# Group norm in token order, and x turned by crossbar DMA, in an attention layer for 64 images

## The chip, the cores and the metric

The kernel runs on one core of a Trainium2 chip. The core has TensorE (PE in the rows; PEld is its weight load), VectorE (DVE), ScalarE (ACT), GpSimd (POOL), SyncE (SP, which here only issues DMAs) and 16 DMA engines. The metric is device time in microseconds (us) of one execution, lower is better.

## What is computed

Group norm over x, attention with LoRA and decomposed relative positions for each of 64 images of 14 x 14 tokens, a projection, and x added on. Cut to what matters:

```python
# x: (64, 14, 14, 768); 12 heads of 64; G = 32 groups of 24 channels
g = x.reshape(64, 14, 14, 32, 24)
m = mean(g, axis=(1, 2, 4)); s = var(g, axis=(1, 2, 4))
t = ((g - m) / sqrt(s + 1e-5)).reshape(x.shape)
qkv = t @ qkv_w.T + qkv_b          # new_q = t @ la_q.T @ lb_q.T is added to q, new_v likewise to v
attn = (q * scale) @ k.T + rel_h(q) + rel_w(q)     # 196 x 196 per image and head
out = x + softmax(attn) @ v @ proj_w.T + proj_b
```

## The kernel before

Images go in pairs (32 rounds, `pairs`), 392 columns each. Products with f32 precision are made of three f16 products (high x high, low x high, high x low), so each operand has a `_hi` and a `_lo` half. `prepare` merges LoRA into the weights and splits them; `attend` is the main loop. It keeps x of one pair in `x_sb` as 98 token partitions x 4 blocks x 768 channels.

What each engine does in which order is written out by hand in the tables `PE_ORDER`, `ACT_ORDER`, `DVE_ORDER`, `SP_ORDER`: an entry (kind, old, k) stands for step k of that kind for the pair of the round less `old` (-1 is the next pair, 1 the one before). Each engine goes through its list in order and waits on semaphores; nothing overtakes. The kinds:

- S k, P k (k = 0 to 11: a pair of heads of one image): score product, and product of probabilities and v. Between them on DVE and ACT: the row maximum (S, L769), exponentials (N on ACT, L682), reciprocal and splitting (N and T, L777 to L789), then a crossbar DMA on SP that turns the split probabilities (`turned<-split`, T, L528).
- Q, K, V k (k = 0 to 5): projections of 18 products (L556), read by ACT and DVE. R: relative positions (L578). Y, Z: output projection (L623), turned back (L629), added to x (`y_sb`, L803); LY and ST load and store `y_sb`, which has YS = 3 slots; `yT` has 2.
- LD (ACT's queue): the load of `x_sb` for a later pair.
- X k (k = 0 to 5): PE turns x, four f32 transposes each (L637); ACT copies them to `xT`, channels on partitions (L708); DVE takes bn_stats of each image (L808).
- M, G: bn_aggr (L813), then two products with `gmean` average over a group's partitions (L642), DVE derives mean and variance; POOL raises to the power -0.5 on [128, 2] (L722).
- H, L: DVE normalizes `xT` (L833), ACT writes `xn_hi` (L712), DVE `xn_lo` (L839). Q 0 of a pair waits for them.

PSUM results other than scores and P go through a ring of 5 banks; a product waits until the result five places before it was read.

## Time and profile before

| | |
|---|---|
| median of 3 runs | 3372.74 us (3370.44 to 3375.27) |
| the profiled execution, its own time | 3373.03 us |
| its span in the trace | 3371.3 us |
| PE, DVE, ACT, POOL busy | 98%, 75%, 62%, 1% of the span |
| queue of SP's DMAs (q1), share of the 16 DMA engines | 49.8% |

The profile is one execution. Busy time of PE is that of overlapping products: a product of 392 columns is listed with 0.33 us, but the next begins 0.17 later. The chain of waits tells the time that each really adds.

### The profile page before, as it was taken

How to read it: one execution, taken by the hardware profiler on the slowest of the kernel's cores; microseconds unless marked ns; L12 is line 12 of the kernel's file. 1: busy time of each engine (PE TensorE's matmuls, PEld its weight loads, DVE VectorE, ACT ScalarE, POOL GpSimd, SP SyncE). 2: the span in 40 equal slices, each digit the busy share in tenths (PEclk: the TensorE clock that was granted, in tenths of full speed). 3: DMA queues.
4: the chain of work that ended last, by engine and by line, in shares of the span. 5: the costliest groups of instructions: out<-in, count | busy, mean ns of one | idle time of the engine just before them, and what ended most of it. 6: DMA issues, size and time to landing. Idle time of an engine off the chain costs nothing.

```text
span 3371.3 us, 80148 instructions
## 1 busy us (share of the span) xinstructions
PE 3297.2 (98%) x31984; PEld 2130.7 (63%) x31984; DVE 2528.2 (75%) x5970; ACT 2098.2 (62%) x5651; POOL 35.8 (1%) x65
## 2 busy tenths in 40 slices
PE   7689999999999999999999999999999999999998
PEld 4456666666666666666666666666666666666665
DVE  7577777777777777777777777777777777777764
ACT  2466666666666666666666666666666666666664
POOL 0000000000000000000000000000000000000000
PEclk9799999999999999999999999999999999999999
DMA  3145664555555556565555555555565555565554
GB/s 128 42 96 109 120 122 103 115 113 112 118 121 107 113 112 114 116 121 107 110 116 113 112 123 118 101 117 111 110 127 120 100 118 108 111 126 122 103 106 105
DMA packets 1091412, 376.13 MB, mean 112 GB/s; under 512 B 916696, under 2 KB 1071320, under 8 KB 1091040
## 3 DMA queue, kind: packets, MB, share of 16 engines
q1 hardware_dynamic: 1075206, 333.63, 49.8%
q10 hardware_dynamic: 15834, 37.37, 3.9%
q8 instruction: 254, 4.16, 0.5%
q14 instruction: 118, 0.97, 0.1%
HBM read 86.60 MB, written 38.54 MB: 37 GB/s over the span
## 4 chain that ended last, share of the span: by engine, by line
PE 94%; DVE 2%; ACT 1%; issue 0%; DMA 0%; POOL 0%; SPq 0%; POOLq 0%; DVEq 0%
PE ring L556 51%; PE ring L623 17%; PE score L599 9%; PE o_ps L613 7%; PE ring L578 3%; PE ring L637 3%; PE ring L629 3%; ACT prob L682 1%; PE ring L642 0%; PE ring L563 0%; DVE split L789 0%; DVE row_max L769 0%; DVE rel_sb L762 0%; DVE split L781 0%; DVE rel_sb L756 0%
## 5 line engine op out<-in xcount | busy, mean ns | idle before, releaser
L556 PE MATMUL ring<-xn_hi,w_hi 128*128 128x392 f16 x3456 | 1143.2, 331 | 4.8 <-DVE xn_lo L839 4.6
L556 PE MATMUL ring<-xn_lo,w_hi 128*128 128x392 f16 x3456 | 1139.8, 330 | 0.0
L556 PE MATMUL ring<-xn_hi,w_lo 128*128 128x392 f16 x3456 | 1139.3, 330 | 0.5 <-issue 0.5
L682 ACT ACTIVATE prob<-score,neg_max,exp_scale 98x196 f32<-98x196 f32 x1536 | 769.8, 511 | 252.9 <-DVE neg_max L773 245.4
L769 DVE TENSOR_REDUCE row_max<-score 98x4 f32<-98x784 f32 x384 | 373.3, 972 | 273.2 <-PE score L599 272.1
L789 DVE SCALAR_TENSOR_TENSOR split<-prob,row_inv,split 98x196 f16<-98x196 f32 x1536 | 545.0, 417 | 7.8
L556 PEld LDWEIGHTS ring<-xn_hi,w_hi 128*128 128x128 f16 x3456 | 342.3, 99 | 260.7 <-issue 7.7
L556 PEld LDWEIGHTS ring<-xn_hi,w_lo 128*128 128x128 f16 x3456 | 338.8, 98 | 237.9 <-issue 3.6
L556 PEld LDWEIGHTS ring<-xn_lo,w_hi 128*128 128x128 f16 x3456 | 338.9, 98 | 208.3 <-issue 1.9
L623 PE MATMUL ring<-o_hi,w_hi 128*128 128x392 f16 x1152 | 380.2, 330 | 1.4 <-DVE o_lo L798 1.4
L623 PE MATMUL ring<-o_lo,w_hi 128*128 128x392 f16 x1152 | 379.8, 330 | 0.0
L623 PE MATMUL ring<-o_hi,w_lo 128*128 128x392 f16 x1152 | 379.6, 330 | 0.0
L690 ACT ACTIVATE split<-prob,row_inv 98x196 f16<-98x196 f32 x768 | 310.3, 456 | 52.9 <-DVE row_inv L777 52.1
L682 ACT ACTIVATION_READ_ACCUMULATOR prob<-score,neg_max,exp_scale 98x1 f32 x1536 | 306.2, 199 | 0.0
L658 ACT ACTIVATE q_hi<-ring,bias 128x392 f16<-128x392 f32 x192 | 112.1, 584 | 297.8 <-PE ring L556 297.8
L777 DVE RECIPROCAL row_inv<-row_sum 98x4 f32<-98x4 f32 x384 | 68.0, 177 | 290.6 <-ACT prob L682 290.6
L613 PE MATMUL o_ps<-turned,v_tok 98*64 98x196 f16 x4608 | 269.5, 252 | 4.0 <-DMA turned<-split 4.0
L701 ACT ACTIVATE yT<-ring,bias,y_scale 128x392 f32<-128x392 f32 x192 | 130.1, 678 | 220.6 <-PE ring L623 220.6
L599 PE MATMUL score<-k_hi,q_hi 64*98 64x196 f16 x1536 | 205.7, 264 | 19.7 <-DVE k_lo L736 12.3
L781 DVE TENSOR_SCALAR split<-prob,row_inv 98x196 f16<-98x196 f32 x768 | 213.0, 320 | 14.3 <-DVE row_inv L777 0.8
L613 PEld LDWEIGHTS o_ps<-turned,v_tok 98*64 98x64 f16 x4608 | 184.8, 109 | 56.1 <-DMA turned<-split 4.3
L697 ACT ACTIVATE o_hi<-o_ps,bias 128x392 f16<-128x392 f32 x192 | 112.7, 587 | 141.3 <-PE o_ps L613 141.3
(118 smaller groups left out, 4896.7 us busy)
## 6 DMA issues: line engine op xcount, KB each, us to landing
y_sb<-in_x SPq DMA_DIRECT2D x192, 196.0 KB
out<-y_sb SPq DMA_DIRECT2D x192, 196.0 KB
x_sb<-in_x ACTq DMA_DIRECT2D x31, 1176.0 KB
rel_q<-rel_sb SPq DMA_DIRECT2D x128, 122.5 KB, 2.4
stage<-in_L_conv_qkv_w SPq DMA_DIRECT2D x3, 2304.0 KB, 15.4
turned<-split SPq DMA_TRANSPOSE x384, 4.2
rel_q<-rel_sb SPq DMA_DIRECT2D x128, 24.5 KB, 1.9
v_tok<-v_split SPq DMA_TRANSPOSE x192, 3.4
```

The costliest lines, as they stand in the source:

```text
L556: last = T.matmul(ring[:, bank, 0:NT], w[:, c, 128 * j:128 * j + 128], xx[:, par, c, :], start=(c == 0 and part == 0), stop=(c == CT - 1 a ...
L599: last = T.matmul(score[0:HALF, head, to], stat[rows, qs], kk[rows, :], start=(part == 0), stop=(part == 3))
L613: last = T.matmul(o_ps[rows, c0:c0 + TOK], v_tok[0:HALF, hp % 2, vv, 2 * image + kh, rows], turned[0:HALF, image, pp, head, :, kh, 0:HALF] ...
L623: last = T.matmul(ring[:, bank, 0:NT], w[:, c, 128 * j:128 * j + 128], oo[:, par, c, :], start=(c == 0 and part == 0), stop=(c == HP - 1 a ...
L658: last = A.activation(to, ring[:, bank, 0:NT], ACT.Identity, bias=bias[:, j:j + 1])
L682: last = A.activation(prob[:, head, half, :], score[0:HALF, head, TOK * half:TOK * half + TOK], ACT.Exp, bias=neg_max[:, k % 2, i:i + 1], ...
L690: last = A.activation(split[0:HALF, k % 2, 0, 0, half, :, 0:HALF], prob[:, 0, half, :].rearrange("p (a k) -> p a k", a=2), ACT.Copy, scale ...
L697: A.activation(o_hi[:, par, hp, :], o_ps[:, 0:NT], ACT.Identity, bias=bias[:, 2 * CT + hp:2 * CT + hp + 1]).then_inc(o_hi_made, 1)
L701: A.activation(yT[:, k % 2, :], ring[:, bank, 0:NT], ACT.Identity, bias=bias[:, 3 * CT + k:3 * CT + k + 1], scale=y_scale[:, :]).then_inc( ...
L769: V.tensor_reduce(row_max[:, k % 2, :], score[0:HALF, :, 0:2 * TOK].rearrange("p a (b k) -> p a b k", b=2), AX.X, ALU.max).then_inc(row_ma ...
L781: last = V.tensor_scalar(split[0:HALF, k % 2, 0, 1, half, :, 0:HALF], prob[:, 1, half, :].rearrange("p (a k) -> p a k", a=2), row_inv[:, k ...
L789: last = V.scalar_tensor_tensor(split[0:HALF, k % 2, 1, head, half, :, 0:HALF], prob[:, head, half, :].rearrange("p (a k) -> p a k", a=2), ...
```

## The change

The statistics are taken in token order, before x is turned, and the turning moves from PE to the DMA queue. A k (k = 0, 1: one image) sums each group's 24 channels of two blocks for each token partition on DVE; product G 0 with `gmean` (now 98 x 98, all 1/(24 x 196)) adds over partitions and leaves the mean on every partition; B k subtracts it in `x_sb`; U k squares on ACT into `squares` (which shares memory with `xs`, as do `qw_hi` and `qw_lo`); D k sums the squares; product G 1 gives the 64 variances on 64 partitions, one element each; POOL takes the power there; E puts them on a diagonal; product G 2 with ones spreads them over the token partitions; H k multiplies `x_sb`; I k (ACT) and L k (DVE) write the f16 halves to `xs`; XT k (k = 0 to 3, SP) turns one image of one half by crossbar DMA into `xn`, and Q 0 waits for all four. `y_sb` has 2 slots and `yT` one, into which ACT writes Y k only after Z k-1. The tables of all engines are written anew around this. A new memset clears `xs` (6144 f16 columns); the tables `rt_hi`, `rt_lo` become narrower with the same content used, and `prepare` turns weights without a strided view.

```diff
-GP = C // GROUPS // CT
+GP = C // GROUPS
...
-YS = 3
+YS = 2
...
+    each("S", 0, 0) + each("P", 1, 10) + each("Z", 2, 5) + each("V", 0, 0) + each("K", 0, 1)
+    + each("S", 0, 1) + each("P", 1, 11) + each("G", -1, 1) + each("V", 0, 1) + each("G", -1, 2) + each("Y", 1, 0)
...
-    + each("X", -2, 0, 1, 2))
+    + each("B", -2, 1) + each("D", -2, 0))
...
+    + each("VT", 0, 1) + each("LY", 1, 1) + each("XT", -1, 0) + each("T", 0, 2)
+    + each("XT", -1, 1, 2) + each("ST", 1, 0) + each("XT", -1, 3) + each("T", 0, 3) + each("LY", 1, 2)
...
         sem = lambda name: own.enter_context(nc.semaphore(name))
-        xT = S("xT", [128, CT, NT], F32)
-        xn_hi = S("xn_hi", [128, 2, CT, NT], F16)
-        xn_lo = S("xn_lo", [128, 2, CT, NT], F16)
-
...
 
         q_hi = S("q_hi", [128, 2, HP, NT], F16)
         q_lo = S("q_lo", [128, 2, HP, NT], F16)
-        columns = xT[:, :, :].bitcast(F16).rearrange("p (t a) (b w h) -> p t (a b) w h", t=2, b=2, w=W)
+        columns = xs[:, :, :, :].rearrange("p a b c -> p (a b c)")[:, 0:2 * HP * NT].rearrange(
+            "p (t a w h) -> p t a w h", t=2, a=HP, w=W)
         qw_hi, qw_lo = columns[:, 0], columns[:, 1]
+        squares = xs[0:HALF].rearrange("p a b c -> p (a b c)").bitcast(F32).rearrange("p (b c) -> p b c", b=4)
...
+                elif kind == "XT":
+                    part, image = k // 2, k % 2
+                    wait(sp, xs_lo_made if part else xs_hi_made, 2 * p + image + 1)
+                    sp.sem_inc(sp_go, 1)
+                    sp.dma_start_transpose(xn[:, p % 2, part, 2 * image:2 * image + 2].rearrange("p b c r -> p (b c) r"),
+                                           xs[0:ROWS, part, 2 * image:2 * image + 2].rearrange("r b c -> r (b c)")
+                                           ).then_inc(xn_in, 16)
...
-                        if kind == "Q" and k == 0 and c % 2 == 0:
-                            wait(pe, xn_lo_made, 3 * p + c // 2 + 1)
-                        for part, (w, xx) in enumerate(((w_hi, xn_hi), (w_hi, xn_lo), (w_lo, xn_hi))):
+                        if kind == "Q" and k == 0 and c == 0:
+                            wait(pe, xn_in, 64 * p + 64)
+                        for part, (w, xx) in enumerate(((w_hi, 0), (w_hi, 1), (w_lo, 0))):
                             last = T.matmul(ring[:, bank, 0:NT], w[:, c, 128 * j:128 * j + 128],
-                                            xx[:, par, c, :], start=(c == 0 and part == 0),
+                                            xn[:, par, xx, :, c, 0:HALF], start=(c == 0 and part == 0),
                                             stop=(c == CT - 1 and part == 2))
...
-                elif kind == "X":
-                    if k == 0:
-                        wait(pe, x_in, 16 * p + 16)
-                    for i in range(4):
-                        src = x_sb[:, i, :].rearrange("p (a b) -> p b a", b=CT)[:, k, :]
-                        last = T.transpose(ring[:, bank, HALF * i:HALF * i + HALF], src, ident[0:HALF, 0:HALF])
+                                           yT[:, HALF * i:HALF * i + HALF], ident[:, :])
                     last.then_inc(done[kind], 1)
                 elif kind == "G":
-                    wait(pe, group_in, 2 * p + k + 1)
-                    src = mean_var[:, :, 0] if k == 0 else spread[:, :]
-                    T.matmul(ring[:, bank, 0:2], gmean[:, :], src, start=True, stop=True).then_inc(done[kind], 1)
+                    if k < 2:
+                        wait(pe, summed, 4 * p + 2 * k + 2)
+                    else:
+                        wait(pe, diagonal_made, p + 1)
+                    both = sums[:, :, :].rearrange("p n g -> p (n g)")
+                    if k == 0:
+                        last = T.matmul(ring[0:HALF, bank, 0:2 * GROUPS], gmean[:, :], both, start=True, stop=True)
+                    elif k == 1:
+                        last = T.matmul(ring[0:2 * GROUPS, bank, 0:1], both, gmean[:, 0:1], start=True, stop=True)
+                    else:
+                        last = T.matmul(ring[0:HALF, bank, 0:2 * GROUPS], ones[:, :], diagonal[:, :], start=True, stop=True)
+                    last.then_inc(done[kind], 1)
 
         @block.scalar
...
                     wait(act, done[kind], 6 * p + k + 1)
-                    A.activation(yT[:, k % 2, :], ring[:, bank, 0:NT], ACT.Identity,
+                    wait(act, done["Z"], 6 * p + k)
+                    A.activation(yT[:, :], ring[:, bank, 0:NT], ACT.Identity,
                                  bias=bias[:, 3 * CT + k:3 * CT + k + 1],
...
-                elif kind == "X":
-                    wait(act, done[kind], 6 * p + k + 1)
-                    if k == 0:
-                        wait(act, xn_lo_made, 3 * p)
-                    A.activation(xT[:, k, :], ring[:, bank, 0:NT], ACT.Copy).then_inc(read["X"], 1)
-                elif kind == "H":
-                    wait(act, normed, 3 * p + k + 1)
+                elif kind == "U":
+                    wait(act, centred, 2 * p + k + 1)
+                    wait(act, done["R"], RCH * p)
                     two = slice(2 * k, 2 * k + 2)
-                    A.activation(xn_hi[:, par, two], xT[:, two, :], ACT.Copy).then_inc(xn_hi_made, 1)
+                    A.activation(squares[:, two], x_sb[:, two, :], ACT.Square).then_inc(squared, 1)
+                elif kind == "I":
+                    wait(act, normed, 2 * p + k + 1)
+                    two = slice(2 * k, 2 * k + 2)
+                    A.activation(xs[0:HALF, 0, two], x_sb[:, two, :], ACT.Copy).then_inc(xs_hi_made, 1)
 
...
+            G.memset(xs[:, :, :, :].rearrange("p a b c -> p (a b c)"), 0.0).then_inc(pads_zeroed, 1)
+            G.memset(ones[:, :], 1.0).then_inc(pads_zeroed, 1)
...
-                wait(pool, read["G"], 2 * p + 2)
-                G.tensor_tensor(rstd[:, :], var_eps[:, :], minus_half[:, :], ALU.pow).then_inc(rstd_made, 1)
+                wait(pool, read["G"], 3 * p + 2)
+                G.tensor_tensor(inv_dev[:, :], var_eps[:, :], minus_half[:, :], ALU.pow).then_inc(inv_dev_made, 1)
...
-                elif kind == "X":
-                    wait(dve, read["X"], 6 * p + k + 1)
-                    for image in range(2):
-                        V.bn_stats(stats[:, image, k, :],
-                                   xT[:, k, TOK * image:TOK * image + TOK]).then_inc(stats_made, 1)
-                elif kind == "M":
-                    wait(dve, stats_made, 12 * p + 12)
-                    V.memset(spread[:, :], 0.0)
-                    V.bn_aggr(mean_var[:, 0, :], stats[:, 0].rearrange("p a b -> p (a b)"))
-                    V.bn_aggr(mean_var[:, 1, :], stats[:, 1].rearrange("p a b -> p (a b)")).then_inc(group_in, 1)
-                elif kind == "G" and k == 0:
-                    wait(dve, done["G"], 2 * p + 1)
-                    V.tensor_copy(mean[:, :], ring[:, bank, 0:2]).then_inc(read["G"], 1)
-                    wait(dve, read["G"], 2 * p + 1)
-
-                    V.tensor_tensor(spread[:, :], mean_var[:, :, 0], mean[:, :], ALU.subtract).then_inc(dev_made, 1)
-                    wait(dve, dev_made, 2 * p + 1)
-                    V.tensor_tensor(spread[:, :], spread[:, :], spread[:, :], ALU.mult).then_inc(dev_made, 1)
-                    wait(dve, dev_made, 2 * p + 2)
-                    V.tensor_tensor(spread[:, :], spread[:, :], mean_var[:, :, 1], ALU.add).then_inc(group_in, 1)
+                elif kind == "A":
+                    if k == 0:
+                        wait(dve, x_in, 16 * p + 16)
+                    two = slice(2 * k, 2 * k + 2)
+                    V.tensor_reduce(sums[:, k, :], x_sb[:, two, :].rearrange("p b (g c) -> p g b c", c=GP),
+                                    AX.XY, ALU.add).then_inc(summed, 1)
+                elif kind == "D":
+                    wait(dve, squared, 2 * p + k + 1)
+                    two = slice(2 * k, 2 * k + 2)
+                    V.tensor_reduce(sums[:, k, :], squares[:, two].rearrange("p b (g c) -> p g b c", c=GP),
+                                    AX.XY, ALU.add).then_inc(summed, 1)
+                elif kind == "G" and k == 1:
+                    wait(dve, done["G"], 3 * p + 2)
+                    V.tensor_scalar(var_eps[:, :], ring[0:2 * GROUPS, bank, 0:1], EPS, None,
+                                    ALU.add).then_inc(read["G"], 1)
+                elif kind == "E":
+                    wait(dve, inv_dev_made, p + 1)
+                    V.tensor_scalar(diagonal[:, :], ident[0:2 * GROUPS, 0:2 * GROUPS], inv_dev[:, :], None,
+                                    ALU.mult).then_inc(diagonal_made, 1)
                 elif kind == "G":
-                    wait(dve, done["G"], 2 * p + 2)
-                    V.tensor_scalar(var_eps[:, :], ring[:, bank, 0:2], EPS, None, ALU.add).then_inc(read["G"], 1)
-                elif kind == "H":
-                    if k == 0:
-                        wait(dve, rstd_made, p + 1)
-                    for image in range(2):
-                        part = xT[:, 2 * k:2 * k + 2, TOK * image:TOK * image + TOK]
-                        last = V.tensor_scalar(part, part, mean[:, image:image + 1], rstd[:, image:image + 1],
-                                               ALU.subtract, ALU.mult)
-                    last.then_inc(normed, 1)
+                    wait(dve, done["G"], 3 * p + k + 1)
+                    to = mean if k == 0 else rstd
+                    V.tensor_copy(to[:, :, :].rearrange("p n g -> p (n g)"),
+                                  ring[0:HALF, bank, 0:2 * GROUPS]).then_inc(read["G"], 1)
+                elif kind in ("B", "H"):
+                    wait(dve, read["G"], 3 * p + (1 if kind == "B" else 3))
+                    by_group = x_sb[:, 2 * k:2 * k + 2, :].rearrange("p b (g c) -> p b g c", c=GP)
+                    of = (mean if kind == "B" else rstd)[:, k:k + 1, :]
+                    V.tensor_tensor(by_group, by_group, of.unsqueeze(3).broadcast_to([HALF, 2, GROUPS, GP]),
+                                    ALU.subtract if kind == "B" else ALU.mult
+                                    ).then_inc(centred if kind == "B" else normed, 1)
                 elif kind == "L":
-                    wait(dve, xn_hi_made, 3 * p + k + 1)
+                    wait(dve, xs_hi_made, 2 * p + k + 1)
                     two = slice(2 * k, 2 * k + 2)
-                    V.tensor_tensor(xn_lo[:, par, two], xT[:, two, :], xn_hi[:, par, two],
-                                    ALU.subtract).then_inc(xn_lo_made, 1)
+                    V.tensor_tensor(xs[0:HALF, 1, two], x_sb[:, two, :], xs[0:HALF, 0, two],
+                                    ALU.subtract).then_inc(xs_lo_made, 1)
```

VectorE, the end of step 11 and step 0 (the stretches behind S 11 and S 0) of one round. Before, `stats<-xT` are the bn_stats of X, `y_sb` is Z:

```order
1546 L789 SCALAR_TENSOR_TENSOR split<-prob,row_inv,split 98x2x98 x4
1547 L808 BN_STATS stats<-xT 128x6 x6
1548 L769 TENSOR_REDUCE row_max<-score 98x4
1549 L773 TENSOR_SCALAR neg_max<-row_max,neg_scale 98x4
1550 L803 TENSOR_TENSOR y_sb<-ring,y_sb 98x512
1551 L808 BN_STATS stats<-xT 128x6 x2
1552 L777 RECIPROCAL row_inv<-row_sum 98x4
1553 L781 TENSOR_SCALAR split<-prob,row_inv 98x2x98 x2
1554 L789 SCALAR_TENSOR_TENSOR split<-prob,row_inv,split 98x2x98 x4
1555 L803 TENSOR_TENSOR y_sb<-ring,y_sb 98x512
```

After, `x_sb<-x_sb,mean` is B 1, `sums<-xs` are D 0 and D 1:

```order
1524 L792 SCALAR_TENSOR_TENSOR split<-prob,row_inv,split 98x2x98 x4
1525 L836 TENSOR_TENSOR x_sb<-x_sb,mean 98x1536
1526 L817 TENSOR_REDUCE sums<-xs 98x32
1527 L772 TENSOR_REDUCE row_max<-score 98x4
1528 L776 TENSOR_SCALAR neg_max<-row_max,neg_scale 98x4
1529 L806 TENSOR_TENSOR y_sb<-ring,y_sb 98x512
1530 L780 RECIPROCAL row_inv<-row_sum 98x4
1531 L784 TENSOR_SCALAR split<-prob,row_inv 98x2x98 x2
1532 L792 SCALAR_TENSOR_TENSOR split<-prob,row_inv,split 98x2x98 x4
1533 L747 TENSOR_TENSOR v_split<-ring,v_split 128x4x98
1534 L806 TENSOR_TENSOR y_sb<-ring,y_sb 98x512
1535 L817 TENSOR_REDUCE sums<-xs 98x32
```

In place of the bn_stats stand one B ahead of the row maximum of S 0 and a D on either side of that step; D 1 is the last of step 0.

TensorE, from P 10 in step 0 to the group products in step 1. Before, with X 3 to 5 (`ident,x_sb`) and the product on the means much later:

```order
6507 L613 MATMUL o_ps<-turned,v_tok 64x196 x12
6508 L629 MATMUL ring<-ident,yT 98x128 x4
6509 L637 MATMUL ring<-ident,x_sb 128x98 x12
6510 L556 MATMUL ring<-xn_hi,w_hi 128x392
...
6572 L623 MATMUL ring<-o_hi,w_lo 128x392
6573 L642 MATMUL ring<-mean_var,gmean 128x2
```

After, `gmean,sums` is G 1 and `diagonal,ones` G 2:

```order
6435 L610 MATMUL o_ps<-turned,v_tok 64x196 x12
6436 L626 MATMUL ring<-ident,yT 98x128 x4
6437 L553 MATMUL ring<-xn,w_hi 128x392 x2
...
6461 L596 MATMUL score<-k_hi,q_hi 98x196 x2
...
6469 L610 MATMUL o_ps<-turned,v_tok 64x196 x12
6470 L638 MATMUL ring<-gmean,sums 64x1
6471 L553 MATMUL ring<-xn,w_hi 128x392 x2
...
6483 L640 MATMUL ring<-diagonal,ones 98x64
6484 L620 MATMUL ring<-o_hi,w_hi 128x392
```

The twelve transposes are gone, and the product on the sums of squares (G 1) stands right behind the P product of step 1, ahead of a V projection; G 2 follows that projection.

## Rows read from the trace of the kernel before

**Rows 1.** Stage table, steady part: window, length, busy of PE, PEld, DVE, ACT, POOL

```profile
240.00:3130.00 2890.00, 2888.16 (x28467) 1868.07 (x28463) 2206.38 (x5266) 1856.22 (x5026) 20.03 (x29) 1.00 0.56 114
```

**Rows 2.** Chain that ended last, one pair: start us, us, engine and line, count

```profile
1604.96 0.80 PE score L599 x16
...
1629.24 0.81 PE score L599 x16
...
1639.60 0.81 PE score L599 x16
...
1641.03 3.09 PE ring L556 x18
1644.12 1.59 PE ring L637 x12
1645.71 2.99 PE ring L623 x18
...
1649.13 0.80 PE score L599 x16
...
1655.72 0.81 PE score L599 x16
...
1663.23 0.12 PE ring L642 x2
...
1664.77 0.34 PE ring L642 x2
...
1705.43 0.80 PE score L599 x16
```

**Rows 3.** VectorE in order of time: start us, us, line, operation, count, idle before

```profile
1616.72 0.18 DVE L777 RECIPROCAL row_inv<-row_sum 98x4 f32<-98x4 f32 x1 [1.10 <-ACT prob L682]
...
1618.86 0.62 DVE L736 SCALAR_TENSOR_TENSOR q_lo<-ring,bias,q_hi 128x392 f16<-128x392 f32 x1
...
1633.76 1.06 DVE L762 SCALAR_TENSOR_TENSOR rel_sb<-ring,rel_scale,rel_part 64x504 f16<-64x504 f32 x1
...
1640.85 0.57 DVE L744 TENSOR_TENSOR v_split<-ring,v_split 128x392 f16<-128x392 f32 x1
1641.34 0.96 DVE L769 TENSOR_REDUCE row_max<-score 98x4 f32<-98x784 f32 x1
...
1644.73 0.18 DVE L777 RECIPROCAL row_inv<-row_sum 98x4 f32<-98x4 f32 x1 [1.04 <-ACT prob L682]
...
1647.28 1.68 DVE L808 BATCH_NORM_STATS2 stats<-xT 128x6 f32<-128x196 f32 x6
...
1673.54 0.69 DVE L803 TENSOR_TENSOR y_sb<-ring,y_sb 98x512 f32<-98x512 f32 x1
```

**Rows 4.** VectorE's groups of instructions: count, busy us, mean ns of one, idle before

```profile
L808 DVE BATCH_NORM_STATS2 stats<-xT 128x6 f32<-128x196 f32 x384 | 112.9, 350 | 18.1 <-ACT xT L708 18.1
...
L839 DVE TENSOR_TENSOR xn_lo<-xT,xn_hi 128x784 f16<-128x784 f32 x96 | 87.6, 968 | 0.0
L833 DVE TENSOR_SCALAR xT<-xT,mean,rstd 128x392 f32<-128x392 f32 x192 | 83.4, 477 | 0.9 <-POOL rstd L722 0.9
...
L316 DVE TENSOR_REDUCE mx<-stage 128x1 f32<-128x4608 f32 x2 | 9.9, 4942 | 0.0
```

**Rows 5.** DMAs: issue of an x load; its queue from 1705 to 1706; turns of `turned`

```profile
1699.50 0.32 ACTq L653 DMA_DIRECT2D x_sb<-in_x  x1
...
q10 hardware_dynamic: 26, 0.04, 13.1%
...
DMA to landing us min/median/max: 4.0/4.2/8.9
```

**Rows 6.** Chain that ended last, at the start of the main loop

```profile
89.69 3.51 POOL split L716
93.20 1.75 POOL v_split L717
...
106.18 20.75 PE ring L556 x108
```

More of the change, by code:

```diff
@@ new lines @@
+    each("Y", 2, 5) + each("U", -1, 1) + soft(0) + each("V", 0, 0)
+    + each("K", 0, 1) + each("P", 1, 11) + soft(1) + each("V", 0, 1)
+    + each("Y", 1, 0) + each("I", -1, 0) + each("N", 0, 2) + each("K", 0, 2) + each("T", 0, 2) + each("I", -1, 1)
+    + each("Y", 1, 1) + each("P", 0, 1) + soft(3) + each("Y", 1, 2)
+    + each("V", 0, 2) + soft(4) + each("K", 0, 3)
+    + each("Q", -1, 0) + each("P", 0, 3) + soft(5) + each("V", 0, 3) + each("LD", -2, 0)
+    + each("Q", -1, 1) + each("N", 0, 6) + each("K", 0, 4) + each("T", 0, 6)
@@ L110 @@
     + each("S", 0, 11) + each("Z", 1, 3) + each("P", 0, 9) + each("N", 0, 11) + each("K", -1, 0) + each("T", 0, 11)
-    + each("X", -2, 0, 1, 2))
+    + each("B", -2, 1) + each("D", -2, 0))
 POOL_ORDER = each("G", -1, 1)
@@ L270, in _ @@
                                  pattern=[[-1, 128]], channel_multiplier=1))
-            step(G.memset(gmean[:, :], 1.0 / GP))
-            view = gmean[:, :].rearrange("p (a b) -> p a b", b=GP)
-            step(G.affine_select(out=view, in_=view, compare_op=ALU.is_ge, fill=0.0, base=0,
-                                 pattern=[[-GP, 128 // GP], [0, GP]], channel_multiplier=1))
-            step(G.affine_select(out=view, in_=view, compare_op=ALU.is_ge, fill=0.0, base=GP - 1,
-                                 pattern=[[GP, 128 // GP], [0, GP]], channel_multiplier=-1))
+            step(G.memset(gmean[:, :], 1.0 / (GP * TOK)))
             step(G.memset(pick[:, :, :], 0.0))
@@ L380, in _ @@
                 for head in range(2):
-                    for at in (32 * head, 32 * head + 16):
+                    for at in (0, 16):
                         rows = slice(64 * head, 64 * head + 64)
@@ L418, in _ @@
                 for i in range(3):
-                    if grp < 3:
-                        src = stage[:, j0 + i, :].rearrange("p (a b) -> p b a", b=CT)[:, t, :]
-                    else:
-                        src = stage[:, j0 + i, 128 * t:128 * t + 128]
-                    last = T.transpose(ring[:, n % 4, 128 * i:128 * i + 128], src, ident[:, :])
+                    last = T.transpose(ring[:, n % 4, 128 * i:128 * i + 128],
+                                       stage[:, j0 + i, 128 * t:128 * t + 128], ident[:, :])
                 last.then_inc(turned, 1)
@@ L466, in attend @@
         row_inv = S("row_inv", [HALF, 2, 4], F32)
-        stats = S("stats", [128, 2, CT, 6], F32)
-        mean_var = S("mean_var", [128, 2, 2], F32)
-        mean = S("mean", [128, 2], F32)
-        spread = S("spread", [128, 2], F32)
-        var_eps = S("var_eps", [128, 2], F32)
-        rstd = S("rstd", [128, 2], F32)
-        minus_half = S("minus_half", [128, 2], F32)
+        sums = S("sums", [HALF, 2, GROUPS], F32)
+        mean = S("mean", [HALF, 2, GROUPS], F32)
+        rstd = S("rstd", [HALF, 2, GROUPS], F32)
+        var_eps = S("var_eps", [2 * GROUPS, 1], F32)
+        inv_dev = S("inv_dev", [2 * GROUPS, 1], F32)
+        minus_half = S("minus_half", [2 * GROUPS, 1], F32)
+        diagonal = S("diagonal", [2 * GROUPS, 2 * GROUPS], F32)
+        ones = S("ones", [2 * GROUPS, HALF], F32)
         ring = own.enter_context(nc.psum_tensor("ring", [128, BANKS, 512], F32))
@@ L534, in _ @@
                 elif kind == "LY":
-                    wait(sp, y_out[k % YS], 32 * p + 16 * (k // YS))
+                    wait(sp, y_out[k % YS], 16 * (CT // YS) * p + 16 * (k // YS))
                     sp.dma_start(y_sb[:, k % YS], x_rows[p][:, :, 128 * k:128 * k + 128]).then_inc(y_in[k % YS], 16)
             for slot in range(YS):
-                sp.wait_ge(y_out[slot], 16 * 2 * pairs)
+                sp.wait_ge(y_out[slot], 16 * (CT // YS) * pairs)
         @block.tensor
@@ L577, in _ @@
                                             "p (g i w) -> p g i w", i=n_rows, w=W)[:, :, i, :]
-                                    last = T.matmul(cols, tab[rows, ax, row, 32 * head:32 * head + 32], mov,
+                                    last = T.matmul(cols, tab[rows, ax, row, :], mov,
                                                     start=(part == 0), stop=(part == 2))
@@ L652, in _ @@
                     if p > 0:
+                        wait(act, xs_lo_made, 2 * p)
                         act.dma_start(x_sb[:, :, :], x_rows[p]).then_inc(x_in, 16)
```

117 lines of the change are left out of this document (52 added, 65 removed).

## The prediction

> **What bounds the kernel now.** I read the stage table first. Over 2890 us of the steady part TensorE is busy for 2888.16, at full clock, VectorE for 2206.38 (76%), ScalarE for 1856.22 (64%) [rows 1]. "Busy" can hide overlap, so the second view is the chain that ended last: from one pair of images to the next it holds nothing but TensorE. Score product 7 of one pair starts at 1604.96, of the next at 1705.43: a pair costs 100.47 us, all of it TensorE work laid end to end [rows 2]. What leaves TensorE shortens the pair; what is put elsewhere is free only as long as no TensorE instruction comes to wait for it. So the third view is VectorE's order of time, because it obeys a fixed order too and takes over most of the new work.
>
> I call "step k" the stretch from score product S k to S k+1. Step 10 is 1639.60 - 1629.24 = 10.36 us, step 11 is 1649.13 - 1639.60 = 9.53, step 0 is 1655.72 - 1649.13 = 6.59 [rows 2]. Score and P products that open a step take 1641.03 - 1639.60 = 1.43, one projection group 3.09 behind them and 2.99 (output) behind other work [rows 2].
>
> **What leaves TensorE.** The six turns of x per pair (X, 24 transposes): two blocks of 1.59 us (1644.12 to 1645.71 is one) [rows 2], so 3.18 per pair. The two small products over groups (0.12 + 0.34 = 0.46 [rows 2]) become three. Nearest price: the 0.34; the new ones are wider (64 columns) but two of them stand between long groups. 3 x 0.34 = 1.02, between 0.46 (nothing extra) and 1.8 (0.6 each). Net: 3.18 - 0.56 = 2.62 less per pair. Projections read x with gaps between the four blocks of 98 tokens; I take no cost, as the number of columns stays 392. If nothing waited, a pair would cost 97.85.
>
> **What VectorE gets.** Out go 12 bn_stats (112.9 us in all), the multiply with mean and 1/deviation (83.4) and the old xn_lo (87.6) [rows 4]: 283.9/32 = 8.9 us per pair. In come ten operations on 98 x 1536: A twice, B twice, D twice, H twice, L twice. None is in the trace. Two rows give a line: 784 elements 0.968, 4608 elements 4.942 [rows 4], that is 1.039 ns per element and 0.968 + 752 x 0.00104 = 1.75 us each. Back to back less is paid: six bn_stats of 0.350 take 1.68 together [rows 3, 4], so 0.08 overlaps each time, and I take 1.67. Ten are 16.7; with copies and the diagonal some 0.8 more. VectorE gains 8.6 us per pair, from 76.7 to about 85 of 98 to 100. It fits on average. The question is where it piles up.
>
> **Where it piles up.** Step 11 now ends on VectorE with B 1 and D 0, step 0 with D 1, and TensorE wants the sums of D 1 for its group product G 1 right behind the P product of step 1; everything on TensorE is in order behind G 1. I follow VectorE from S 10, counting from TensorE's start of it (1629.24):
> - Step 10 does almost the same before and after: one R more in it, but that one runs while ScalarE works on the next, and the end is set by the exponentials and R 3, R 4 behind them, as before. Row maximum 11 began at 1641.34, so at 12.10, directly behind the v_split work without a gap [rows 3]; TensorE had finished S 11 some 0.9 earlier.
> - From a row maximum to the reciprocal 1644.73 - 1641.34 = 3.39 pass (VectorE waits for the exponentials and does short things meanwhile); reciprocal to the end of the splitting with a K in it 1647.28 - 1644.73 = 2.55, without one 1618.86 - 1616.72 = 2.14 [rows 3].
> - Step 11: 12.10 + 3.39 + 2.55 + 2 x 1.67 = 21.38. Row maximum 0 begins there.
> - Step 0: 21.38 + 3.39 + 2.14 + 0.49 (V, 1641.34 - 1640.85) + 0.69 (Z) [rows 3] + 1.74 for D 1 = 29.83.
> - TensorE meanwhile: 10.36 + (9.53 - 1.59) + (6.59 - 1.59 + 2.99, as K 1 moves in for an X block) + 1.43 = 27.72 [rows 2].
> So TensorE waits 29.83 - 27.72 = 2.11 us for G 1, in every pair. Behind it VectorE is late by no more than its step 1 exceeds TensorE's (3.39 + 2.14 + a copy, V and H, 0.2 + 0.49 + 1.67 = 7.9 against 1.43 + 0.34 + 3 + 0.34 + 3 = 8.1), that is not at all, and steps 2 to 5 hold less. In 6 to 8 the sums and B of the pair after come. On VectorE step 6 is 3.39 + 2.55 + 1.67 = 7.61, step 7 3.39 + 2.14 + 0.49 + 1.67 = 7.69, step 8, with a Q read of two operations like V's, 3.39 + 2.14 + 0.98 + 1.67 = 8.18; TensorE's are 1.43 + 3.09 + 2.99 = 7.51, 7.51 and, with a group product, 7.85. That is a lag of 0.6 to 0.8, which step 9, longer on TensorE by two R products, takes back before S 10. The load of x must land before A 0: issued after V 3 in step 5, some 9 us ahead; in the trace a load is issued at 1699.50 and in the microsecond from 1705 its queue moves its last 0.04 of 1.2 MB [rows 5]. Covered by 3 us.
>
> **The pair.** 100.47 - 2.62 + 2.11 = 99.96, a gain of 0.51. TensorE is full in about 30 of the 32 rounds (the first has no output projection, the last no next pair): 30 x 0.51 = 15 us gained, made of 79 us won and 63 lost again.
>
> **The front.** ScalarE and VectorE wait for GpSimd's memsets; 4096 columns take 3.51 from 89.69, and v_split 1.75 behind it; the new 6144 columns take 5.27. The first Q product starts at 106.18, that is 11.2 after the memsets' end [rows 6]. After, its chain is: A A, B B, H H, L L (4 x 3.42 = 13.7), a square on ScalarE and D 1 (1.6 + 1.74), three products with their reads, the power and the diagonal (3.2), and the last turn of x, nearest row 4.2 [rows 5]: 24.4. So Q starts at 94.96 + 5.27 + 24.4 = 124.6, 18.5 later. Pair 1's sums then wait for its load in the middle of the Q products, about 3 more (0 to 5). Front: 22. The first round is set by VectorE's chain rather than TensorE: 2 (0 to 8). In the tail one yT and two y_sb slots instead of three chain the last output groups: 1 (0 to 3).
>
> **The sum.** On the profiled execution (3373.03 us, 0.3 above the median of the runs): 3373.0 - 15 + 22 + 2 + 1 = 3383.
>
> **A rule against the change.** TensorE turns 98 columns of x in 1.59/12 = 0.13 us, while one crossbar turn of 16 blocks lands after 4.2 [rows 2, 5]. The Trainium skill, "VectorE: DVE Perf Modes", section "Rules for kernel authors", sends a 128 x 128 transpose to TensorE if PSUM is an acceptable destination and to the crossbar otherwise. By that rule the 3.18 us per pair would stay where they are; by the rows they sit on the only full engine, while a DMA turn uses none of it as long as it arrives in time.
>
> **Rivals.**
> 1. No wait at G 1 (faster). The chain must be 2.1 us shorter: the three large operations in it would have to run at about 1.0 us each, or splitting and exponentials overlap more than in my sum. Against it: no single row shows a rate below 1 ns per element for this kind of two-operand or summing work. For it: the sum crosses three steps, and an error of 7% in 30 us undoes it. Time: 3383 - 30 x 2.11 = 3320; halfway, 3351.
> 2. Grouped access is dear (slower). The 32 groups of 24 need a broken-up view or a broadcast operand. The row of an operation with a strided view, 504 elements in 1.06 [rows 3], lies 0.38 above the line's 0.68, or 0.76 ns per element. At that price each large operation costs 1.2 more, three of them 3.5, and the pair 103.5: 3383 + 30 x 3.5 = 3488. Inner runs here are 24 contiguous elements, nearer to the contiguous rows; a third of the price gives 3418.
> 3. The turned x is late (slower). The last turn is issued some 4.9 + 0.5 us into step 3 and Q 0 starts 7.9 + 5.0 = 12.9 into it: 3.6 beyond a landing of 4.2. Four turns stand in one queue with those of the probabilities, whose slowest took 8.9 [rows 5]; at that duration Q 0 waits some 1.0: 3383 + 30 = 3413.
> 4. The change not doing what it says can't be: the order of instructions shows the X products gone. What can be is that only the front is dearer and the wait half: that is within my forecast.
>
> **Chances.** Forecast 0.50, its own range 3366 to 3400 (front 16 to 30, wait 1.7 to 2.5). Rival 1: 0.27. Rival 2: 0.13. Rival 3: 0.10. A measurement of this kernel tells about 0.2% (7 us) from no change. Of the forecast 0.18 lies within it and 0.32 above. Faster 0.27, same 0.18, slower 0.55. Range: 3325, most of rival 1, to 3412, leaving out most of rival 2.
>
> **What would show it.** TensorE's waits must name one line, the group product on the sums, behind VectorE's tensor_reduce over xs, about 30 times and 2.1 us each (some 63 in all); a pair must take about 100.0; VectorE's large operations 1.75 us; the first Q near 124.6. Without that wait, or with the reduce below 1.2 us, rival 1 holds; with reduces or multiplies above 2.0, rival 2; with the wait at the first Q product behind the DMA of xn, rival 3. The sum is wrong as a whole if TensorE's own work per pair is not near 97.9.

## The result, and the profile after

| | before | after |
|---|---|---|
| median of 4 runs | 3372.22 us | 3414.14 us (3414.05 to 3417.9) |
| ratio | | 1.0126, 95% interval 1.0109 to 1.0144 |
| the profiled execution, its span | 3373.03, 3371.3 us | 3414.05, 3412.3 us |
| PE, DVE busy, share of the span | 98%, 75% | 95%, 81% |

The change makes the kernel 42 us slower. The forecast was 3383, slower by 10; the direction is right, the size is 31 us short, and the time lies 2 us outside the range.

First, TensorE's waits in the kernel after (line of the waiting product, what released it, us in total, times, longest):

```profile
PE ring L638 <- DVE sums L817: 68.2, 31, 7.5
PE ring L636 <- DVE sums L812: 25.2, 32, 18.2
...
PE ring L553 <- DMA xn<-xs: 12.4, 2, 11.7
```

L638 is G 1 behind VectorE's reduce over the squares, L636 is G 0, L553 Q 0 behind the turned x. Less the one of 7.5 us, G 1 waits 60.7 us in 30 rounds, 2.02 each. Q 0 waits for a turn only twice, 11.7 us of it in front of the main loop. G 0 waits another 7.0 us behind the 18.2 in front. So the large wait is the one forecast. The sum over the waits, though, doesn't explain the time, and that is the first sign that something else is paid.

VectorE's new groups (busy us, mean ns of one, idle before), which answer to [rows 4]:

```profile
L836 DVE TENSOR_TENSOR x_sb<-x_sb,rstd 98x1536 f32<-98x1536 f32 x64 | 111.9, 1750 | 0.0
L842 DVE TENSOR_TENSOR xs<-x_sb,xs 98x1536 f16<-98x1536 f32 x64 | 111.9, 1749 | 0.0
L836 DVE TENSOR_TENSOR x_sb<-x_sb,mean 98x1536 f32<-98x1536 f32 x64 | 111.8, 1749 | 0.0
L812 DVE TENSOR_REDUCE sums<-x_sb 98x32 f32<-98x1536 f32 x64 | 111.5, 1744 | 11.9 <-POOL ones L720 10.8 <-DMA x_sb<-in_x 1.0
L817 DVE TENSOR_REDUCE sums<-xs 98x32 f32<-98x1536 f32 x64 | 111.4, 1742 | 0.3 <-ACT xs L709 0.3
```

All five kinds take the 1.75 us forecast, with the broadcast operand and the view by groups of 24 or without.

What the waits don't show stands in the chain that ended last. Two rounds, at G 1 (start us, us, engine and line, count):

```profile
1584.57 1.67 DVE sums L817
1586.37 0.25 PE ring L638 x2
1586.62 3.09 PE ring L553 x18
1589.71 0.31 PE ring L640 x2
1590.02 3.09 PE ring L620 x18
...
1684.64 1.67 DVE sums L817
1686.45 0.25 PE ring L638 x2
1686.70 4.77 PE ring L553 x18
1691.47 0.31 PE ring L640 x2
1691.78 3.09 PE ring L620 x18
```

The same 18 products of V 1 (L553) take 3.09 us in one round and 4.77 in the next; everything else is alike. The stage table says why. Its columns are the window, its length, busy time of PE, PEld, DVE, ACT and POOL, then the granted TensorE clock, DMA share and GB/s. First the round at 1586, then the one at 1686:

```profile
1584.00:1586.00 2.00, 0.21 (x6) 0.00 (x0) 2.00 (x2) 0.59 (x1) 0.00 (x0) 1.00 0.63 119
1586.00:1588.00 2.00, 1.63 (x11) 1.07 (x12) 1.96 (x6) 0.59 (x3) 0.50 (x1) 1.00 1.08 210
1588.00:1590.00 2.00, 2.00 (x14) 1.06 (x12) 1.08 (x5) 1.75 (x8) 0.04 (x1) 1.00 1.34 90
...
1684.00:1686.00 2.00, 0.49 (x12) 0.27 (x8) 2.00 (x3) 0.59 (x1) 0.00 (x0) 1.00 0.59 111
1686.00:1688.00 2.00, 1.55 (x8) 0.94 (x9) 1.96 (x6) 0.51 (x3) 0.42 (x1) 0.77 1.05 203
1688.00:1690.00 2.00, 2.00 (x8) 0.88 (x6) 1.08 (x5) 1.75 (x9) 0.12 (x1) 0.50 0.89 215
1690.00:1692.00 2.00, 2.00 (x11) 1.03 (x10) 1.97 (x7) 1.13 (x3) 0.00 (x0) 0.87 0.14 41
1692.00:1694.00 2.00, 2.00 (x14) 1.17 (x12) 2.00 (x3) 0.01 (x1) 0.00 (x0) 1.00 0.44 82
```

In the second round the granted clock falls from 1.00 to 0.50 (from 2.4 to 1.2 GHz) just behind the idle stretch and comes back some 4 us after G 1 started. In the stage table over 2890 us it hardly shows:

```profile
240.00:3130.00 2890.00, 2817.26 (x27728) 1752.14 (x27717) 2402.49 (x4801) 1875.99 (x4858) 15.70 (x29) 0.99 0.65 127
```

0.99 against 1.00 in [rows 1]. PE's busy time has fallen by 70.9 us. Those are the waits for G 1 and G 0 and some short ones, not a gain. Slowed products count as busy, so this row hides what they cost.

How often? POOL takes its power once in each pair, just behind G 1, so the intervals between its starts are the lengths of the rounds:

```profile
1587.50 0.54 POOL L725 TENSOR_TENSOR inv_dev<-var_eps,minus_half 64x1 f32<-64x1 f32 x1 [101.22 <-DVE var_eps L821]
1687.58 0.54 POOL L725 TENSOR_TENSOR inv_dev<-var_eps,minus_half 64x1 f32<-64x1 f32 x1 [99.54 <-DVE var_eps L821]
1789.34 0.54 POOL L725 TENSOR_TENSOR inv_dev<-var_eps,minus_half 64x1 f32<-64x1 f32 x1 [101.22 <-DVE var_eps L821]
```

1687.58 - 1587.50 = 100.08, and 1789.34 - 1687.58 = 101.76. Of the 30 intervals 12 are 100.06 to 100.32, 17 are 101.72 to 101.80, and the first, 95.03, is the incomplete round. Nothing lies between. The same intervals of the kernel before are 100.47 to 100.49 in nearly all rounds.

### The profile page after: what moved, and what is told of

Read it like the earlier page. It is cut to its first block, busy times and chain, and to the rows that moved or that the text cites. A ratio compares the mean times of both kernels' runs of the same rounds, so it can differ in the third digit from the quotient of the medians.

```text
span 3412.3 us, 78575 instructions
## 1 busy us (share of the span) xinstructions
PE 3239.4 (95%) x31280; PEld 2010.3 (59%) x31280; DVE 2759.5 (81%) x5490; ACT 2127.6 (62%) x5491; POOL 35.2 (1%) x65
## 4 chain that ended last, share of the span: by engine, by line
PE 58%; DVE 26%; ACT 9%; issue 3%; DMA 1%; SPq 0%; POOL 0%; DVEq 0%; ACTq 0%; POOLq 0%
PE ring L553 32%; PE ring L620 12%; ACT prob L682 7%; DVE split L792 6%; PE score L596 5%; PE o_ps L610 4%; DVE sums L812 3%; DVE sums L817 3%; DVE row_max L772 3%; PE ring L575 2%; DVE x_sb L836 2%; DVE rel_sb L765 2%; DVE split L784 2%; PE ring L626 1%; DVE v_split L747 1%
## 5 line engine op out<-in xcount | busy, mean ns | idle before, releaser
L553 PE MATMUL ring<-xn,w_hi 128*128 128x392 f16 x6912 | 1736.7, 332 | 12.4 <-DMA xn<-xs 12.4
L553 PE MATMUL ring<-xn,w_lo 128*128 128x392 f16 x3456 | 1146.8, 332 | 0.0
L553 PEld LDWEIGHTS ring<-xn,w_hi 128*128 128x128 f16 x6912 | 649.7, 97 | 495.0 <-issue 27.1
L553 PEld LDWEIGHTS ring<-xn,w_lo 128*128 128x128 f16 x3456 | 335.5, 97 | 250.6 <-issue 13.6
L596 PE MATMUL score<-onehot,rel_q 64*98 64x196 f16 x1536 | 191.0, 245 | 0.0
L596 PE MATMUL score<-k_lo,q_hi 64*98 64x196 f16 x1536 | 190.9, 245 | 0.0
L596 PE MATMUL score<-k_hi,q_lo 64*98 64x196 f16 x1536 | 190.8, 244 | 0.0
```

The costliest lines, as they stand in the source:

```text
L553: last = T.matmul(ring[:, bank, 0:NT], w[:, c, 128 * j:128 * j + 128], xn[:, par, xx, :, c, 0:HALF], start=(c == 0 and part == 0), stop=(c ...
L596: last = T.matmul(score[0:HALF, head, to], stat[rows, qs], kk[rows, :], start=(part == 0), stop=(part == 3))
```

## Experiments

The question: are the missing 31 us the clock that falls behind the wait, and what would the change be worth without the wait? The first runs tell the clock apart from the other things that are new in the same microseconds (transfers, reading xn with gaps), the later ones go after the wait itself. Step numbers are those of the prediction; ratios are against the kernel before. All rows of this section follow the columns explained above.

| run | what it is | us | ratio, 95% interval | wait behind P 11 or o_lo, us per pair | rounds, us |
|---|---|---|---|---|---|
| after | the change | 3414.1 | 1.0109 to 1.0144 | 2.0 | 12 of 100.1, 17 of 101.76 |
| fill | 11 products in the wait | 3389.6 | 1.0029 to 1.0063 | 0.15 or less, once 0.38 | 100.02 to 101.1 |
| fill5 | 5 products in the wait | 3383.0 | 1.0022 to 1.0048 | 1.0 | 27 of 30 are 100.03 to 100.06 |
| before_wait | wait in the old kernel | 3475.1 | 1.0286 to 1.0317 | 2.59 | 16 of 103.1, 13 of 104.8 |
| before_half | a shorter one | 3430.6 | 1.0154 to 1.0185 | 1.79 | 102.30 |
| short | less work on VectorE, part of the statistics left out | 3320.4 | 0.9829 to 0.9858 | 0 | 97.70 to 98.9 |
| late | G 1 and G 2 later | 3365.4 | 0.9968 to 0.9986 | 1.40 | 99.20 to 100.4 |
| late4 | and o_lo earlier | 3326.3 | 0.9844 to 0.9877 | 0 | 97.73 to 98.8 |
| late5 | and G 0 later, memset on VectorE | 3311.9 | 0.9802 to 0.9832 | 0 | 97.60 to 98.4 |

### The wait filled with work: fill and fill5

```diff
+                    if k == 1:
+                        for _ in range(11):
+                            T.matmul(ring[:, bank, 0:NT], w_hi[:, 0, 0:128], w_hi[:, 0, 0:NT], start=True, stop=True)
                     if k < 2:
                         wait(pe, summed, 4 * p + 2 * k + 2)
```

(5 instead of 11 in fill5.)

> The changed kernel with eleven more products of 392 columns on TensorE, in front of its wait for G 1; they write into G 1's ring bank, which G 1 overwrites, so the output is the same. They run inside the wait of about 2.2 us and are a load that nothing needs. Theory (what my sum lacked, about 31 us, is the lower granted clock behind the wait, in 18 or 19 of the 31 rounds with 1.7 us each): TensorE has hardly a gap any more, the clock stays at 1.00 behind G 1, every round takes 100.1 us, and the kernel 3414 - 19 x 1.68 = 3382 us, although it does more work. Rival (the V projection behind G 1 is slow in those rounds for another reason, such as the transfers that run at that time, or its reading of xn with gaps): the rounds of 101.7 us stay, and the time is 3414 us or more. If the eleven products end later than the sums come, up to 0.3 us per round are to be added: 3391.

Measured: 3389.6 us, 24.6 less than the changed kernel, with more work on TensorE. No interval of 101.7 us was left. Some rounds took 100.3 to 101.1, where the expectation gave 100.1 for all; the spare products can outlast the arrival of the sums, and that is paid: in 12 of them G 1 starts 0.2 to 1.0 us after the sums are there, where 0.05 is the usual. The time lies inside the 3382 to 3391 expected. The rival, that V 1 is slow because of the transfers beside it or of its own reading, falls. Both are unchanged in this run.

> Run fill with five instead of eleven extra products ahead of the wait for G 1. They take 5 x 0.17 = 0.83 us, so TensorE still waits about 1.4 us in every pair, all of it as one gap. Run fill took 3389.6 us, some 7 us above 100.1 us per round, because now and then the products end after the sums have come. Runs late (gap 1.40 us) and before_half (1.8 us) had no loss of clock. Theory (what counts is the length of the gap, and a gap of 1.4 us costs nothing beside itself): all rounds 100.1 us, 3414 - 19 x 1.68 = 3382 us, less than run fill with less work in the gap. Rival (the clock is kept only by an engine busy throughout): rounds of two kinds again, 3390 to 3414 us.

Measured: 3383.0 us. The waits of TensorE still name G 1 (its line is L641 here):

```profile
PE ring L641 <- DVE sums L820: 35.0, 31, 5.8
```

35.0 less the front's 5.8 is 29.2 us in 30 rounds by this view, which gives about 1.0 where 1.4 was expected, and the rounds are 100.03 to 100.06 in 27 of 30, none above 100.6. So TensorE need not be busy throughout. Five useless products bring back the whole 31 us. The rival of this run, rounds of two kinds, falls.

### The wait alone, in the kernel before: before_wait and before_half

```diff
+        extra = S("extra", [HALF, 1], F32)
...
 PE_ORDER = (
...
-    + each("S", 0, 1) + each("P", 1, 11) + each("K", 0, 1) + each("Y", 1, 0) + each("G", -1, 0)
+    + each("S", 0, 1) + each("P", 1, 11) + each("W", 0, 0) + each("K", 0, 1) + each("Y", 1, 0) + each("G", -1, 0)
...
 DVE_ORDER = (
...
-    + each("V", 0, 0) + each("S", 0, 1) + each("P", 1, 11) + each("X", -1, 5) + each("M", -1, 0)
+    + each("V", 0, 0) + each("W", 0, 0) + each("S", 0, 1) + each("P", 1, 11) + each("X", -1, 5) + each("M", -1, 0)
...
+                elif kind == "W":
+                    wait(pe, extra_made, p + 1)
...
+                elif kind == "W":
+                    V.tensor_reduce(extra[:, :], w_hi[0:HALF, 0, 0:1536], AX.X, ALU.max).then_inc(extra_made, 1)
```

(0:768 in before_half.)

> The kernel before, nothing of the change in it, but with a wait put in: VectorE does one more maximum over 98 x 1536 f16 elements at the end of step 0 (nothing uses it), and TensorE waits for it behind the P product of step 1, where G 1 stands in the changed kernel. In the kernel before VectorE is some 1 us behind TensorE there, so with the 1.7 us of the new operation TensorE waits about 2.4 us per pair (1.5 to 3). Theory (the clock falls behind such a wait whatever the kernel): rounds of two kinds, some without and some with 1.7 us more, the granted clock below 1.00 just behind the wait in a part of the rounds, and 3372 + 31 x 2.4 = 3446 up to 3446 + 31 x 1.7 = 3500 us. Rival (the loss belongs to what the change brought, the turned x or its transfers): the wait alone, rounds of one length, 3446 us, or 3420 to 3465 by the bounds of the wait.

Measured: 3475.1 us, inside 3446 to 3500. Of 29 complete intervals 16 are 103.1 us and 13 are 104.8. The chain of two rounds, with the old kernel's projection (here L557) behind the wait:

```profile
1704.29 1.67 DVE extra L809
...
1706.01 3.16 PE ring L557 x18
1709.17 2.98 PE ring L624 x18
...
1807.40 1.67 DVE extra L809
...
1809.11 4.84 PE ring L557 x18
1813.95 2.98 PE ring L624 x18
```

and the stage table of the second:

```profile
1808.00:1810.00 2.00, 0.89 (x6) 0.55 (x7) 1.96 (x3) 0.00 (x0) 0.00 (x0) 1.00 1.10 222
1810.00:1812.00 2.00, 2.00 (x9) 0.99 (x8) 1.75 (x7) 1.77 (x7) 0.00 (x0) 0.57 0.65 170
1812.00:1814.00 2.00, 2.00 (x9) 0.98 (x8) 0.73 (x3) 0.34 (x3) 0.00 (x0) 0.58 0.28 83
1814.00:1816.00 2.00, 2.00 (x14) 1.18 (x13) 1.39 (x4) 1.27 (x3) 0.00 (x0) 1.00 0.00 0
```

There is no turned x, no xn with gaps and no G 1 in this kernel, and the loss is the same 1.68 us (4.84 - 3.16). It comes with the wait.

> Run before_wait with the extra maximum over 768 instead of 1536 elements, so that the wait put into the kernel before is shorter by some 0.8 us: about 1.8 instead of 2.6 us per pair. Run late had a wait of 1.40 us in every pair and no round with a loss of clock; the changed kernel has 2.2 us and a loss in 18 of 30 rounds. Without any loss the time is 3373 + 31 x 1.8 = 3429 us and all rounds have one length; with 1.68 us lost in half of them it is 3455 us. I hold both for possible and expect rounds of two kinds, since 1.8 is nearer to 2.2 than to 1.4.

Measured: 3430.6 us; rounds of 102.30, 26 of 30 intervals within 0.01 of it. One is 1.4 higher, the third, and so it is in the kernel before without any wait (101.90 for 100.48). That is 100.48 + 1.82: the wait and nothing else. I had expected rounds of two kinds; that miss stands. TensorE's waits of the two runs:

```profile
PE ring L557 <- DVE extra L809: 81.5, 32, 2.8
...
PE ring L557 <- DVE extra L809: 56.0, 32, 2.0
```

So 0.8 us more of wait cost 3475.1 - 3430.6 = 44.5 us instead of 31 x 0.8 = 25. The 13 rounds with a loss, 13 x 1.69 = 22 us, are the rest.

### Less work on VectorE: short

The first two lines are those of D, the rest those of B and H.

```diff
-                    two = slice(2 * k, 2 * k + 2)
+                    two = slice(2 * k, 2 * k + 1)
...
+                    n_b = 1 if kind == "B" and k == 1 else 2
-                    by_group = x_sb[:, 2 * k:2 * k + 2, :].rearrange("p b (g c) -> p b g c", c=GP)
+                    by_group = x_sb[:, 2 * k:2 * k + n_b, :].rearrange("p b (g c) -> p b g c", c=GP)
```

> The changed kernel with less work on VectorE: B 1 subtracts the mean from one block of two, and D 0 and D 1 sum the squares of one block of two. Left out is thus a part of the statistics and of the normalization; the shapes of everything else and TensorE's order are the same. VectorE's chain ahead of G 1 is shorter by three times 768 elements at about 1.04 ns, 2.4 us. Theory (TensorE's wait is exactly VectorE's chain through steps 11 and 0, and the lost clock hangs on the wait): no wait at G 1, no loss of clock, a pair of 97.8 to 98.1, and 3312 to 3325 us. Rival (the wait at G 1 comes from elsewhere, ScalarE's squares or the exponentials): the wait stays above 1 us and the time above 3370.

Measured: 3320.4 us, inside 3312 to 3325. TensorE waits for the sums of squares only in front of the main loop:

```profile
PE ring L638 <- DVE sums L817: 6.4, 1, 6.4
```

and the shortest rounds are 97.7 us, G 0's wait of 0.2 included, where 97.85 was forecast for TensorE's work alone. With VectorE's chain through steps 11 and 0 some 2.4 us shorter, nothing of the wait at G 1 is left.

### G 1 where its sums are there: late, late4, late5

Run late, step 1 in TensorE's table:

```diff
-    + each("S", 0, 1) + each("P", 1, 11) + each("G", -1, 1) + each("V", 0, 1) + each("G", -1, 2) + each("Y", 1, 0)
+    + each("S", 0, 1) + each("P", 1, 11) + each("V", 0, 1) + each("G", -1, 1) + each("Y", 1, 0) + each("G", -1, 2)
```

> The changed kernel with TensorE's order alone altered: G 1 stands behind the V projection of step 1 instead of ahead of it, G 2 behind the output projection Y 0. VectorE's order is the same. Theory (both the wait of 2.2 us and the 1.7 us of lost clock hang on the place of G 1): TensorE has 3 us of work ahead of G 1 and waits for nothing there, the clock stays at 1.00, a pair takes 97.8 to 98.0 us, and the kernel 3414 - 30 x 2.2 - 19 x 1.7 = 3316 us. Rival (VectorE's chain through steps 11 and 0 is what binds, and lateness is carried on): the wait turns up again 5 to 12 us later, at the first score or P product of step 2, or at Q 0 behind the turned xn; at a full 2.2 us per round, without or with the loss of clock, that is 3382 to 3414.

Measured: 3365.4 us, the first version of the change that is faster than the kernel before (0.9968 to 0.9986), but 49 above the theory's 3316. The rival got a part: the wait was not carried on by 5 to 12 us, but to the very next reader of VectorE. TensorE's waits:

```profile
PE ring L620 <- DVE o_lo L801: 43.6, 31, 1.6
```

and the chain:

```profile
1664.90 0.22 PE ring L638 x2
...
1665.14 0.15 DVE var_eps L821
1665.29 0.53 DVE k_lo L739
1665.83 0.54 DVE o_lo L801
...
1666.50 3.15 PE ring L620 x18
```

Y 0 needs o_lo of P 11, which stands on VectorE behind D 1, the row maximum of S 1 and K 1. G 1's wait had covered that lateness. The gap of 1.40 us costs just itself: rounds of 99.21 and none above 100.42, and the V projection ahead of it at 3.09.

Run late4 has this beside it, step 1 in VectorE's table:

```diff
-    + each("S", 0, 1) + each("G", -1, 1) + each("K", 0, 1) + each("P", 1, 11) + each("E", -1, 0) + soft(1)
+    + each("P", 1, 11) + each("S", 0, 1) + each("G", -1, 1) + each("K", 0, 1) + each("E", -1, 0) + soft(1)
```

> The kernel of run late (G 1 behind the V projection, G 2 behind Y 0 on TensorE) with one more step moved: on VectorE the reading of P 11 (o_lo) stands ahead of the row maximum of S 1 instead of behind K 1. In run late the wait of 2.2 us had come down to 1.40 us at Y 0, behind o_lo, with the clock at 1.00 and pairs of 99.21 us; VectorE finished o_lo at 1666.37 there and would now at 1665.3, with TensorE ready at 1665.1. Theory (no other thing is late once o_lo comes first): 0.2 us of wait, pairs of 97.75 + 0.2 to 98.2 us, 3365 - 31 x 1.15 = 3330 us, from 3318 to 3335. Rival (the exponentials of step 1, begun 0.55 us later, now make a P or score product late): a wait at P or S in steps 2 or 3, 0.5 us or more in a pair, and 3345 us or more.

Measured: 3326.3 us, inside the 3318 to 3335 of the theory, 47 below the kernel before. The chain at this place is TensorE alone again:

```profile
1743.59 3.09 PE ring L553 x18
1746.69 0.21 PE ring L638 x2
1746.89 3.09 PE ring L620 x18
1749.98 0.22 PE ring L640
```

Run late5 has two more edits, in step 8 of TensorE's table and in the memset of xs:

```diff
-    + each("S", 0, 8) + each("P", 0, 6) + each("G", -2, 0) + each("Q", -1, 4, 5)
+    + each("S", 0, 8) + each("P", 0, 6) + each("Q", -1, 4) + each("G", -2, 0) + each("Q", -1, 5)
...
-            G.memset(xs[:, :, :, :].rearrange("p a b c -> p (a b c)"), 0.0).then_inc(pads_zeroed, 1)
+            V.memset(xs[:, :, :, :].rearrange("p a b c -> p (a b c)").bitcast(U32), 0).then_inc(pads_zeroed, 1)
```

> Run late4 with two small things beside it: on TensorE G 0 stands behind the projection Q 4 of step 8 instead of ahead of it (it waited 0.22 us in each pair), and the memset of xs in front of the main loop is done by VectorE instead of GpSimd (5.15 us there, with VectorE and ScalarE waiting). Theory: 31 x 0.22 = 7 us less per run and 3 to 5 us less in front: 10 to 12 us below run late4, about 3319 us. Rival (the wait at G 0 moves to Q 5 or S 9, and the memset is as long on VectorE): within 3 us of late4.

Measured: 3311.9 us, 14.4 below late4 where 10 to 12 were expected, and 1.8% faster than the kernel before. G 0's wait fell from 26.1 us in 32 places to the one in front:

```profile
PE ring L636 <- DVE sums L812: 13.1, 1, 13.1
```

The memset, 5.15 us on GpSimd, takes 2.62 on VectorE as 3072 words of 32 bits, beside GpSimd's others. (The Trainium skill, "VectorE: DVE Perf Modes", section "Zero memsets can be issued as uint32 (trn2)", has a memset cost by the element whatever its type, so that zeros are best written in words of 4 bytes. The row has 0.85 ns per word; no run here clears f16 elements on VectorE, so that the words are what saves the time is not shown.) The waits at G 0, in front and in the rounds, account for 13.0 us of the 14.4; the rest I have not traced.

## Why the prediction was off

By its own steps:

- **What leaves TensorE.** Right within 0.25 us. 97.85 us per pair if nothing waits; the shortest rounds of short and late4 are 97.70 and 97.73, with G 0's wait in them, those of late5, without it, 97.60.
- **What VectorE gets.** Right. 1.75 us per large operation, measured 1.742 to 1.750; rival 2 (grouped access dear) is refuted by those rows.
- **Where it piles up.** Right in place and size: forecast 2.11 us at G 1 behind D 1, measured 2.02. The sum over three steps held to 0.1 us, and term by term: in the round whose S 10 starts at 1556.50, row maximum 11 begins 12.20 us later (forecast 12.10), row maximum 0 21.46 (21.38), and D 1 ends 29.74 (29.83). Rival 1 (no wait) is refuted by the same wait.
- **Steps 6 to 8 and the load.** Nothing was late there; G 0's wait of about 0.22 us per pair, however, was taken as nothing and cost 7 us a run (25.2 - 18.2). That the pair without loss still came out at 100.07 for the 99.96 forecast is luck in part: this 0.22 too little stands against the 0.25 too much in TensorE's own work.
- **Turned x (rival 3).** Refuted: Q 0 waits twice, and a turn lands after 3.8 us in the median, 5.7 at most, not 8.9.
- **The front.** Forecast +22: the first Q at 124.6, found at 124.38; the first score product of the first pair starts at 165.71 instead of 144.61, 21.1 later. The memset of 5.27 took 5.15.
- **First round and tail.** Forecast +2 and +1, found -1.0 and +4.5: from the first score product of pair 0 to that of pair 1 it is 93.5 us instead of 94.55, from that of the last pair to the end 119.9 instead of 115.4. Both terms were mis-sized, and the sum, 3.5 for 3, is right by luck. Ahead of the last Z the chain now waits 2.31 us for a store and 2.60 for a load of `y_sb`, which has two slots now.
- **The pair.** This is the step that failed. "TensorE waits 2.11 us" was turned into a cost of 2.11 us, with every product behind it at the speed of [rows 2]. Forecast 99.96; the rounds without loss are 100.07, and 17 of the 29 complete ones are 101.76. 17 x 1.69 = 29 us of the 31 missing are in those intervals alone; one more loss, behind G 1 at 3202.83 (4.51 for 3.09), adds 1.4. From the first score product of pair 1 to that of pair 30 the kernel was to win 15 us and lost 14.

The forecast is therefore the time of the changed kernel with its clock held: fill5, which has five useless products more and differs in nothing else, takes 3383.0 us. That the two agree to the microsecond is luck, by the errors above that cancel.

Why did the sum not have it? In the steady part of the kernel before TensorE never idles: [rows 1] show 2888 of 2890 us busy at 1.00. No row there could price a gap, so the sum should have given it an unknown price with two ends. One end is the gap itself. For the other, the kernel before had two hints that the prediction didn't use. One is in its own [rows 6]: 108 products behind the idle front take 20.75 us, where six groups at 3.09 are 18.5; the granted clock from 106 to 127 is 0.87. The other is the window in front of the steady part in the stage table:

```profile
90.00:240.00 150.00, 119.76 (x1187) 77.65 (x1188) 97.81 (x228) 79.51 (x203) 6.42 (x5) 0.88 0.32 69
```

Where TensorE idled for 30 of 150 us, its granted clock was 0.88. A term "a projection group behind the gap at half speed", by an estimate from the 3.09 of [rows 2] 3.1 us more in each round, would have put the upper end at 3383 + 30 x 3.1 = 3476, and the range would have held the time.

What stays open: which round loses the clock. The idle time just ahead of G 1 is not the same in all rounds, and its length does not decide. Two rounds of the changed kernel, first TensorE in order of time (in brackets the idle time before, and what ended it), then the chain behind:

```profile
1181.03 0.25 PE L638 MATMUL ring<-gmean,sums 98*64 98x1 f32 x2 [1.74 <-DVE sums L817]
...
3002.69 0.25 PE L638 MATMUL ring<-gmean,sums 98*64 98x1 f32 x2 [1.74 <-DVE sums L817]
```

```profile
1181.28 4.77 PE ring L553 x18
...
3002.94 3.09 PE ring L553 x18
```

The same gap of 1.74 us stands ahead of a round with loss and of one without. Over the 29 rounds the gaps with a loss behind them are 1.74 to 2.39 us, those without 1.26 to 2.19. In before_wait every gap is 2.59 us and 13 of 29 have a loss, so a longer gap was not followed by one more often than one of 2.1. In before_half, with 1.79 in every complete round, none has, and in late, with 1.40, none either. So a loss was seen behind gaps from 1.74 us up, and no safe length above 1.40 is shown. Nor do the losses fall at random. In the changed kernel one or two rounds with a loss and one without take turns up to the last three, in before_wait one with and one or two without, but for one place. What sets this order, and whether it is the moment at which the gap comes, was not tested; neither was what TensorE does ahead of the gap.

## What to carry to other kernels

Where one engine is full, an instruction of it that waits for a busy neighbour should stand behind work that is ready. Moving two products and one read (two lines of the order tables) turned this change from 1.3% slower to 1.4% faster, with no work removed. After such a move ask at once what the old wait had covered: here it was the next reader of the same engine, 1.4 us behind. And a gap in a full TensorE can have a second price beside its length, which the busy time does not show and a mean clock of 0.99 hardly does; look for the same instruction group with two durations in the chain, and at the granted clock in windows of 2 us.
